# LayerNorm's token turns and the router logits moved behind the query jobs of three groups, in a cross-attention and mixture-of-experts kernel

## The reference

```
x = x + Attention(layernorm(x), context)       # 16 heads of 64; softmax over 1601 keys; output projection + bias
x = x + FFN(layernorm(x))                      # router: sigmoid(tokens @ Wr.T) + bias,
                                               #   2 of 4 groups, then 4 of 32 experts, weights normalised, times 2.5
                                               # 32 experts of width 64 (silu(gate) * up, down), and one shared expert
```

## Time and profile before

| | |
|---|---|
| median of three runs | 3330.06 us (3328.31 to 3333.57) |
| the profiled execution | 3335.48 us, of which the span from first to last instruction is 3333.5 us |
| mean granted TensorE clock | 0.997 |
| attention loop | about 47 to 2991 us of the span |
| expert part | about 3002 us to the end |

### The profile page before, as it was taken

One profiled execution on the slowest core, in us unless ns is written; L12 is line 12 of the kernel. 1 busy time (PEld: TensorE's weight loads), 2 busy tenths in 40 slices (PEclk: granted clock), 3 DMA queues, 4 the chain that ended last, 5 costly groups with the idle time before them and its releaser, 6 DMA issues.

```text
span 3333.5 us, 50432 instructions
## 1 busy us (share of the span) xinstructions
PE 3287.3 (99%) x15589; PEld 2619.0 (79%) x15589; DVE 2401.6 (72%) x4954; ACT 1936.7 (58%) x2239; POOL 1061.6 (32%) x724
## 2 busy tenths in 40 slices
PE   7999999999999999999999999999999999999999
PEld 6777777777777777877777777777777777777887
DVE  5777777777777777777777777777777777777655
ACT  4566556665556565656555656555565556655554
POOL 4222232222332223322223222233222332225555
PEclk9999999999999999999999999999999999999999
DMA  2000000000000000000000000000000000010000
GB/s 90 1 16 1 17 1 10 7 1 17 1 16 1 17 1 16 1 1 17 1 16 1 17 1 16 1 16 2 1 16 1 17 1 16 1 45 4 7 7 10
DMA packets 8682, 35.98 MB, mean 11 GB/s; under 512 B 1657, under 2 KB 2306, under 8 KB 8130
## 3 DMA queue, kind: packets, MB, share of 16 engines
q1 hardware_dynamic: 8386, 32.29, 3.1%
HBM read 29.92 MB, written 2.10 MB: 10 GB/s over the span
## 4 chain that ended last, share of the span: by engine, by line
issue 71%; POOL 18%; PE 9%; DVE 1%; POOLq 0%; ACT 0%; DMA 0%; DVEq 0%; ACTq 0%
POOL p_lo L390 12%; POOL cT_lo L379 2%; PE st L625 2%; POOL v_lo L381 2%; PE st L626 2%; PE st L627 2%; POOL cT_hi L371 1%; POOL v_hi L372 1%; PE op L625 1%; PE op L627 1%; PE op L626 1%; PE side L672 1%; POOL rstd L309 1%; DVE gu_mul L1118 0%; POOLq L389 0%
## 5 line engine op out<-in xcount | busy, mean ns | idle before, releaser
L755 ACT ACTIVATE p_full<-st 128x1024 f32<-128x1024 f32 (+1 forms) x832 | 855.4, 1028 | 1164.6 <-PE st L516 1160.2
L1027 DVE TENSOR_REDUCE m_part<-side 128x1 f32<-128x402 f32 x2048 | 1094.5, 571 | 544.8 <-PE side L460 544.8
L390 POOL TENSOR_TENSOR p_lo<-p_full,p_hi 128x1024 fp32r<-128x1024 f32 x256 | 649.5, 2537 | 2097.1 <-ACT p_hi L758 2097.1
L758 ACT ACTIVATE p_hi<-st 128x1024 fp32r<-128x1024 f32 (+1 forms) x832 | 850.7, 1023 | 0.0
L1015 DVE TENSOR_TENSOR p_lo<-p_full,p_hi 128x1024 fp32r<-128x1024 f32 (+1 forms) x576 | 700.3, 1216 | 141.4 <-ACT p_hi L758 117.9
L460 PE MATMUL side<-cT_hi,qT_hi 96*128 96x402 f32 x2048 | 563.1, 346 | 0.0
L510 PE MATMUL st<-qT_hi,cT_hi 97*128 97x512 f32 (+1 forms) x1668 | 539.9, 405 | 2.9 <-DMA qT_hi<-m_row 2.9
L524 PE MATMUL op<-p_hi,v_hi 128*97 128x512 f32 (+1 forms) x1664 | 527.6, 398 | 6.0 <-DVE p_lo L1015 6.0
L513 PE MATMUL st<-qT_lo,cT_hi 96*128 96x512 f32 (+1 forms) x1668 | 528.0, 397 | 0.0
L516 PE MATMUL st<-qT_hi,cT_lo 96*128 96x512 f32 (+1 forms) x1668 | 523.6, 395 | 0.0
L527 PE MATMUL op<-p_lo,v_hi 128*97 128x512 f32 (+1 forms) x1664 | 519.5, 393 | 0.0
(11 more groups left out here) (146 smaller groups left out, 2636.4 us busy)
## 6 DMA issues: line engine op xcount, KB each, us to landing
keys_nat<-in_ctx_keys SPq DMA_DIRECT2D x18, 624.0 KB, 5.7
keys_tur<-in_ctx_turned SPq DMA_DIRECT2D x18, 603.0 KB, 4.8
out_x<-x SPq DMA_DIRECT2D x8, 256.0 KB, 2.0
x<-in_x SPq DMA_DIRECT2D x1, 1920.0 KB, 12.1
w_rest<-in_moe_w SPq DMA_DIRECT2D x1, 1152.0 KB, 7.2
qT_hi<-m_row SPq DMA_DIRECT2D x65, 4.0 KB
w_first<-in_moe_w SPq DMA_DIRECT2D x1, 960.0 KB, 4.7
aw<-in_attn_w SPq DMA_DIRECT2D x2, 448.0 KB, 5.3
```

The costliest lines, as they stand in the source:

```text
L390: pool.tensor_tensor(p_lo[:, slot(s), :], p_full[:, s % 2, :], p_hi[:, slot(s), :].bitcast(F32), ALU.subtract).then_inc(s_lo_pool, 1)
L755: act.activation(p_full[0:m, s % 2, :], both(st[0:m, s % 2]), ACT.Exp, scale=SCALE)
L758: act.activation(p_hi[0:m, slot(s), :], both(st[0:m, s % 2]), ACT.Exp, scale=SCALE).then_inc(s_ex, 1)
L1027: dve.tensor_reduce(m_part[:, at:at + 1], where[:, 0:MAXW], AX.X, ALU.max).then_inc(s_drain, 1)
```

## The change

The three extra jobs move. L goes to group 1, N stays in group 2, R stays in group 3, and each now stands at t = 12 behind the two Q jobs, which is the last thing before `pv(11)`. ACT does its part behind `queries_hi`, DVE behind `queries_lo`. With that the small steps are spread: `token_stats` of two tiles in group 3 and two in group 0, `normalise` of two tiles in group 0 and two in group 1, and POOL's `deviations` twice a batch, in groups 0 and 1. The first batch's `token_stats` stands ahead of the loop. `x1` grows by two tiles, which POOL sets to zero at the start.

```diff
-        EXTRA = {2: {5: "L", 6: "N"}, 3: {5: "R"}}
+        EXTRA = {1: "L", 2: "N", 3: "R"}
         def places(i):
-            return {t: (a, b + EXTRA.get(i, {}).get(t, "")) for t, (a, b) in PLACES.items()}
+            return {t: (a, b + EXTRA.get(i, "") if t == S - 1 else b) for t, (a, b) in PLACES.items()}
...
-            pool.memset(x1[:, T + 2:T + 4, :], 0.0).then_inc(s_const, 1)
+            pool.memset(x1[:, T + 2:T + 6, :], 0.0).then_inc(s_const, 1)
...
-                            if s == 3 and i == 1:
-                                deviations(bb * 2 + (par + 2), slice(0, 4))
+                            if s == 3 and i < 2:
+                                deviations(bb * 4 + (2 * par + 2 + i), slice(2 * i, 2 * i + 2))
...
                 for s in range(1, S):
                     exp(s)
-                    extra = EXTRA.get(i, {}).get(s)
-                    if extra:
-                        ...
                 for k in range(2):
                     j = job_at[i]["Q"][k]
                     queries_hi(bank(jobs0 + j), jobs + (j + 1), k, i % 2)
+                extra = EXTRA.get(i)
+                if extra:
+                    ...
+                        tokens_hi(where, 1 - par, filled)
...
             carry()
+            token_stats((4, 5), 0)
...
-                    if i in (0, 1):
-                        tiles = [dve.snap(bb * 4 + (2 * par + q)) for q in (4, 5, 0, 1)]
+                    if i != 2:
+                        tiles = [dve.snap(bb * 4 + (2 * par + q)) for q in {0: (4, 5, 0, 1), 1: (0, 1), 3: (6, 7)}[i]]
                     if i == 0:
+                        normalise(tiles[0:2], 0, bb * 4 + (2 * par + 2))
                         dve.wait_ge(s_drain, jobs + (job_at[i]["Y"][-1] + 1))
-                        token_stats(tiles, 0, links)
+                        carry()
+                        token_stats(tiles[2:4], 2, links)
                     elif i == 1:
-                        normalise(tiles, 0, bb * 2 + (par + 2))
+                        normalise(tiles, 2, bb * 4 + (2 * par + 3))
                         route_groups(links)
                     elif i == 2:
                         route_weights(bass.ds(bb * 4 + 2 * par, 2), links)
                     else:
+                        token_stats(tiles, 0, links)
                         route_scores(links)
```

More of the change, by code:

```diff
@@ L54, in sem @@
             return stack.enter_context(nc.semaphore(name))
-        x1 = sb(stack, "x1", [P, T + 4, D])
+        x1 = sb(stack, "x1", [P, T + 6, D])
         ident = sb(stack, "ident", [P, P])
@@ L397, in _ @@
                                 piece_lo(bb, par, i)
-            deviations(B + 2, slice(2, 4))
+            deviations(2 * B + 3, slice(2, 4))
             after_attention(pool)
@@ L561, in side_jobs @@
                         elif kind == "L":
-                            turn_tokens(where, bb * 2 + (par + 2), 0)
+                            turn_tokens(where, bb * 4 + (2 * par + 2), 0)
                         elif kind == "N":
-                            turn_tokens(where, bb * 2 + (par + 2), 2)
+                            turn_tokens(where, bb * 4 + (2 * par + 3), 2)
                         elif kind == "R":
@@ L617, in _ @@
             pe.wait_ge(s_drain, JOBS_END + GH - 1)
-            turn_tokens(bank(JOBS_END + GH), B + 2, 2)
+            turn_tokens(bank(JOBS_END + GH), 2 * B + 2, 2)
             pe.wait_ge(s_drain, JOBS_END + GH + 1)
@@ L778, in body @@
                     queries_hi(bank(jobs0 + j), jobs + (j + 1), k, i % 2)
+                extra = EXTRA.get(i)
+                if extra:
+                    j = job_at[i][extra][0]
+                    where, filled = bank(jobs0 + j), jobs + (j + 1)
+                    if extra == "L":
+                        tokens_hi(where, 1 - par, filled)
+                    elif extra == "N":
+                        act.wait_ge(s_fill, filled)
+                        keep_x2(where, bass.ds(bb * (2 * NQ) + par * NQ, NQ))
+                    else:
+                        keep_exponentials(where, filled)
             with act.Fori(0, B // 2) as bb:
@@ L1069, in body @@
                 after_jobs()
-            links_per_turn = 46
+            links_per_turn = 50
             with dve.Fori(0, B // 2) as bb:
@@ L1093, in _ @@
             after_attention(dve)
-            normalise((T, T + 1), 2, B + 2)
+            normalise((T, T + 1), 2, 2 * B + 2)
             for q in range(2):
```

## The result

| | before | changed |
|---|---|---|
| median, five runs each | 3333.25 us | 3387.95 us (3384.0 to 3388.16) |
| ratio of the runs | | 1.0163, 95% interval 1.0151 to 1.0174 |
| span of the profiled execution | 3333.5 us | 3386.0 us |
| mean granted TensorE clock | 0.997 | 0.997 |

The change costs 1.6%: 54.7 us by the medians, 52.5 us by the two profiled spans. The forecast was 3383.5 us, 53.4 us more. Of the 4.4 us between forecast and median, 3.2 lie in the median it started from (3330.1 us of three runs, 3333.25 of five), and 1.3 in the forecast difference.

A forecast was written before the change was run, and what follows sets the result against it. TensorE was taken to bound the kernel. Moved jobs +54.9 us, back edge -1.8 and head +0.3 gave +53.4 us on 3330.1 us, so 3383.5 us, range 3366 to 3400 us.

The forecast's parts named there:

- The bound: Whole kernel: TensorE is busy 3287 of 3333 us, so only whether it works or waits longer counts.
- The stall: At the ends of groups 1, 2 and 3, TensorE waits 1.43 us for the first `queries_lo`, 48 times.
- The lengths of the groups: Pace of the four groups in the changed kernel: 45.5, 47.1, 47.1 and 47.3 us.
- The back edge: At the loop's back edge, TensorE's wait before `pv(0)` shrinks by 0.25 us, seven times: -1.8 us.
- The rest: Other engines and places count nothing, except the head, where POOL clears four tiles instead of two: +0.3 us.
- The clock falls in the stalls: Rival: behind the 48 new stalls TensorE's clock drops, 2.2 us each, 106 us, about 3490 us; 5 in 100.
- The other side, no stall and N's wait gone: Rival: the first `queries_lo` ends before TensorE reaches the turn, so only work stays: -10 us, 3320 us; 3 in 100.
- No change in time, through a hidden wait at `scores(0)`: Rival: TensorE already waits at `scores(0)` for the last exp, which absorbs the stall: about 3330 us; 2 in 100.
- More cost through late VectorE or ScalarE steps: Rival inside the forecast's 88 in 100: they are late for the next group's first steps; upper end 3400 us.

The follow-up runs named there:

- e6: The kernel of e5 with route_scores moved from the end of group 3 to the end of group 0 of the next batch: 3315.8 us, ratio 0.9945.
- e2: The kernel before, nothing moved, one wait for the first query job's drain added ahead of pv(11) in groups 1, 2 and 3: 3397.3 us, ratio 1.0188.
- e3: The changed kernel, but VectorE drains the first query job ahead of lo(12) and not behind it: 3367.0 us, ratio 1.0099.
- e4: The changed kernel, but TensorE makes the extra job behind pv(11) and not ahead of it: 3336.9 us, ratio 1.0011.
- e1: The changed kernel with L, N and R back at their old places, only the small steps of VectorE and POOL spread: 3338.7 us, ratio 1.0013.
- e8: The kernel of e1 with job L alone moved behind the query jobs of group 1: 3362.8 us.
- e5: The kernel before with job N in group 2 at t = 3 and not at t = 6: 3320.1 us, ratio 0.9958.

## Why the prediction was right

**The bound.** That TensorE's order decides and nothing else was borne out from both sides: its matmuls' busy time stayed within 5 us, and in e6, where the last waits are gone, it shows no idle time in 2910 us.

**The stall.** Forecast 1.43 us in 48 places, released by the first `queries_lo`; measured 1.46 us for a turn and 1.38 us for R, with line 890 as releaser in all 48. e2 has the same 1.45 us with no job moved, e3 moves it with VectorE's drain, e4 takes it away with `pv(11)` as cover. That the wait causes the cost is therefore shown, not only argued.

**The lengths of the groups.** Forecast 45.5, 47.1, 47.1 and 47.3 us; measured 45.50, 47.12, 47.10 and 47.32. A batch is 187.04 us against 183.51 (45.48, 46.66, 45.89 and a fourth of 45.48), 3.53 us more where I had 3.43, so 56.5 us in sixteen batches against 54.9. Of the difference of 0.10 us, 0.02 lie in the three moved jobs (5.04 against 5.02) and 0.08 in the plain length under all four groups (45.50 against 45.48).

**The back edge.** Forecast -1.8 us, measured 8.3 us of waits before and 5.3 now, -3.0 us. The sign was right, the size was not. The timeline of the changed kernel there:

```profile
1543.99 0.17 DVE L930 TENSOR_TENSOR g_sum<-top 128x8 f32<-128x8 f32 x1
...
1547.17 1.23 DVE L1016 TENSOR_TENSOR p_lo<-p_full,p_hi 128x1024 fp32r<-128x1024 f32 x1 [3.00 <-issue]
...
1548.45 0.25 PEld L524 LDWEIGHTS op<-p_hi,v_hi 128*97 128x97 f32 x2 [0.73 <-DVE p_lo L1016]
```

I had carried over 3.38 us from the last step to `lo(0)`; here it is 3.00 us, and that is 0.38 of the 0.51 us by which TensorE's wait shrank in this place (from 1.24 to 0.73, where I had 0.99). The other part, VectorE's later end against TensorE's later arrival, I had put at 0.25 us; by these rows it is 0.14: TensorE was ready for `pv(0)` 3.42 us behind VectorE's last step before and is ready 3.56 us behind it now. So two sizes were off in opposite directions, and that the total misses by only 1.2 us is in part luck.

**The rest.** The first turn of the head starts at 8.7 us instead of 8.5 (0.3 expected). Added up, 56.5 - 3.0 + 0.2 = 53.7 us; the spans differ by 52.5 us and the medians by 54.7.

**The rivals.** *The clock falls in the stalls*: in the changed kernel it did not. The window with one of the stalls' restarts, in the changed kernel, has a granted clock of 1.00:

```profile
1633.00:1637.00 4.00, 3.54 (x17) 2.72 (x18) 3.31 (x15) 0.58 (x2) 0.00 (x0) 1.00 0.01 4
```

Waits of 1.4 to 1.5 us lie with the 1.24 us of the earlier trace rows and not with the 2.9 us of the earlier trace rows, so the throttled default of which the Trainium skill (TensorE: Matmul & The Clock Gate, "What's actually happening") speaks cost nothing in this change. The rival's mechanism is real all the same, and nearer than I had it: of seventeen waits of 1.65 to 1.93 us at the back edge in e1, e4 and e8, four were followed by a stretch at the lower clock, which cost 1.6 us of a pass of the loop in e1 and 0.7 to 2.7 us in e4. The stalls of the changed kernel, at most 1.5 us in the load rows of the loop, lay below these. *The other side, no stall and N's wait gone*: it did not happen in this change, but its mechanism is real. e5 reaches it with one entry of the table, 15 us faster than before, where I had priced N's wait at 10 us in that rival. *No change in time, through a hidden wait at `scores(0)`*: e2 excludes it, since a bare stall ahead of `pv(11)` arrives in full. *More cost through late VectorE or ScalarE steps*: not in the changed kernel; in e4 ScalarE is late at the back edge.

The medians of e5 gain 15 us where the shorter group explains 12; the difference is inside the interval. The spans differ by 15.3 us: 12.5 of them lie between the first and the last of POOL's pauses in the loop, 1.5 ahead of the first (78.69 and 77.14 us) and 1.3 behind the last. The first pause comes at 77.1 to 78.8 us in the ten kernels, whatever was edited, so the rest is most likely scatter of the head and the end; no run isolates it. It was not tried whether e4's place works with the small steps of the kernel before, which would take `token_stats` away from the back edge.

## What to carry to other kernels

On an engine that never idles, ask of each moved job what its wait reaches back to and what is queued behind it. With two banks, a job waits for the drain of the job two places ahead, so it belongs behind work that covers this drain, and not directly behind two other jobs. Work that hides another engine's latency, like `pv(11)` here, has to stay ahead of the new wait; with the three jobs one call later the kernel was 51 us faster.

## What the runs showed of the hardware

The loop's back edge has a price on VectorE and on ScalarE. VectorE needed 3.38 us from its last step to its first in the kernel before and 3.00 us in the changed one; ScalarE needed 3.09 us in e4, where its last step had waited for TensorE, but in the kernel before it started its next exp with a pause of only 2.3 us behind its last step, and TensorE released that one. A reading of this is that the time counts from when the engine's queue passes its last wait and not from the end of its last instruction; no run here isolates that. What is shown is that 2 us less of VectorE's work ahead of the back edge (e6) removes TensorE's wait there, and that a ScalarE step that waits late puts 1.0 to 1.9 us there (e4).

The granted clock stayed at 1.00 through the loop of the changed kernel and of e2, each with 48 waits of 1.4 to 1.5 us, and behind back-edge waits of up to 1.5 us in e4. Behind waits of 1.65 to 1.93 us it fell in one of seven places in e1, in all three of e4, and in none of seven in e8. What decides between them no run here shows.
